# Expert passes rewritten: routing weights copied over the partitions by DMA, gate activated in its bank, norm on ScalarE, routing chain moved

## The chip, the cores and the metric

The kernel runs on one core of a Trainium2 chip. The core has TensorE (PE; its weight loads are listed as PEld), VectorE (DVE), ScalarE (ACT), GpSimd (POOL), SyncE (SP, which here only issues DMAs), 16 DMA engines, an SBUF of 128 partitions and a PSUM of 8 banks (128 partitions x 512 fp32 each). The metric is device time in microseconds of one execution; less is better.

## The reference

Six sublayers work on x, 4 x 1024 tokens of 128 features in fp32, each on a layer norm of x and added to x:

```python
x = x + 0.5 * L0_ffn(ln(x))    # pass ffn0a
x = x + L0_attn(ln(x))
x = x + 0.5 * L0_ffn(ln(x))    # pass ffn0b
x = x + 0.5 * L1_ffn(ln(x))    # pass ffn1a
x = x + L1_attn(ln(x))         # gated unit
x = x + 0.5 * L1_ffn(ln(x))    # pass ffn1b
```

The change is to the four expert passes. L0_ffn has 16 experts of 64 hidden units and a shared expert; L1_ffn has 8 experts of 256. Both compute every expert for every token and weight it by the router:

```python
# L0: scores = sigmoid(x @ gate_w.T); the best 2 of 4 groups, in them the best 4 experts
h = silu(x @ w1[e].T) * (x @ w3[e].T)
y = sum over e of comb[t, e] * (h @ w2[e].T)     # + shared expert, weight 1
# L1: softmax over 8 experts, the best 2, normalized; the same sum with w_gate, w_up, w_down
```

## The kernel before, in words

`phase_moe` (L184) is one pass. It takes the 4096 tokens in 8 groups of 512 (G). Tokens lie on the free axis, hidden units on the partitions, in chunks of 128: NC = 9 chunks in layer 0 (two experts a chunk; the last is the shared expert), 16 in layer 1 (two chunks an expert). Every fp32 product is made of three fp32r matmuls (high x high, high x low, low x high), so each operand is split in a high and a low half.

For chunk c of a group, `up_and_gate` (L302) has three matmuls for the gate, three for the up projection, and one more (L319): a constant selector `sel` times `combt`, the routing weights with experts on the partitions. It spreads each expert's weights over the partitions of its hidden units, in a PSUM bank; in layer 1 only each second chunk has it. ACT takes the silu of the gate from PSUM to SBUF (`silu`, L407); DVE multiplies it with the spread weights (`scale`, L606) and the up projection (`hide`, L614); ACT rounds the result to its high half (`high`, L415), POOL subtracts for the low half (`low`, L461); PE projects down with three matmuls, two chunks later (`project`, L323). ACT has `silu` of chunk c ahead of `high` of c-1. Gate, up and spread weights have two PSUM banks each, y one, and one bank, `misc`, serves every transpose.

Beside the chunks of group g runs a chain for group g+1: DVE's statistics (`stats`, `aggr`), POOL's reciprocal root (`invert`, L455), DVE's `norm` (L509), PE's `turn` (four transposes), ACT's `xh`, DVE's `xl`, the router's `logit` on PE, `lout` on ACT, `lturn` on PE, the selection `r1` to `r4` on DVE (with a tanh on ACT), PE's `cturn` and ACT's copy to `combt`. `r4` writes the weights in a high and a low half (`cstack`). For group g-1, `yout` (ACT), `yturn` (PE) and `add` (DVE, L598) bring y into x. Each engine's program is in order. The dictionary `slot` (L244) says behind which chunk each step of the chain stands; an instruction waits there if its input isn't ready. Groups 2 to 5 of a pass run in a hardware loop of two groups a turn.

SP is idle in the passes, but for weights of the next layer (`SplitAhead`, L1148: all pieces are loaded at the start of the pass; ACT and POOL split them in groups 0, 1, 6 and 7) and the stores of the last pass. In the attention SP copies rows of queries and keys from SBUF to SBUF: L1043 takes 32 rows of `att_parts`, three planes each, to 96 rows; L1057 8 rows, three planes, to 24 rows. In setup, `sel` is loaded and rounded by POOL (L163).

Of the kernel before, what the change touches and what calls it, by code (L numbers as in the profile page):

```python
# [34 lines left out]
ARENA = 13568  # L35
AHEAD = 704
# [7 lines left out]
def pack_layout():  # L44
    at, lay = 0, {}
    for name, n in (("ident", P), ("causal", P), ("causalT", P), ("qsign", 1), ("qlow", 1), ("ksign", 1),
                    ("klow", 1), ("kone", 1), ("outside", P), ("sel0", C0 * P), ("sel1", E1 * P),
                    ("cos", S), ("sin", S)):
        lay[name] = (at, at + n)
        at += n  # L50
    return lay, at

def constants():
# [46 lines left out]
def phase_setup(nc, k, t, a):  # L101
# [3 lines left out]
    with ExitStack() as ctx:  # L105
# [12 lines left out]
        raw_sel, raw_att = sb("raw_sel", [P, C0 * P]), sb("raw_att", [P, 3, P])  # L118
# [20 lines left out]
        def _(act):  # L139
# [4 lines left out]
            act.dma_start(raw_sel[:], a["consts"][:, slice(*lay["sel0"])]).then_inc(consts_in, 16)  # L144
# [9 lines left out]
            act.wait_ge(consts_in, 32)  # L154

        @block.gpsimd
        def _(pool):
# [4 lines left out]
            pool.wait_ge(consts_in, 32)  # L162
            pool.tensor_copy(k.sel[:], raw_sel[:])  # L163
# [5 lines left out]
        def _(dve):  # L169
# [10 lines left out]
            dve.wait_ge(consts_in, 32)  # L180
# [3 lines left out]
def phase_moe(nc, k, tag, layer, turn_no, ahead=None, out=None):  # L184

# [15 lines left out]
    with ExitStack() as ctx:
# [8 lines left out]
        st, mv, veps, rstd = sb("st", [P, TG, 6]), sb("mv", [P, TG, 2]), sb("veps", [P, TG]), sb("rstd", [P, TG])  # L211
        xn, xh_sb, xl_sb = sb("xn", [P, TG, D]), sb("xh", [P, 2, G], F32R), sb("xl", [P, 2, G], F32R)
# [4 lines left out]
        top_sb, pen, hs, df = (sb("top", [P, TG, 8]), sb("pen", [P, TG, 4]), sb("hs", [P, TG, 1]),  # L217
                               sb("df", [P, TG, E1]))
        cstack, combt = sb("cstack", [P, TG, P]), sb("combt", [P, 2, G], F32R)
        sil, scl, hid = sb("sil", [P, 2, G]), sb("scl", [P, 2, G]), sb("hid", [P, 2, G])  # L220
        hid_h, hid_l, y_t = sb("hid_h", [P, 2, G], F32R), sb("hid_l", [P, 2, G], F32R), sb("y_t", [P, G])

        gate_ps, up_ps, comb_ps = k.banks[:, 0:2, :], k.banks[:, 2:4, :], k.banks[:, 4:6, :]
        y_ps, misc = k.banks[:, 6, :], k.banks[:, 7, :]
        misc3 = misc[:].rearrange("p (t c) -> p t c", c=P)

# [4 lines left out]
        logits_t, logits_out, logits_turned, logits_read = (sem(s) for s in  # L231
            ("logits_t", "logits_out", "logits_turned", "logits_read"))
        route = sem("route")
        tanh_done = sem("tanh_done")
        comb_turned, comb_t = sem("comb_turned"), sem("comb_t")
        y_out, y_turned, y_added = sem("y_out"), sem("y_turned"), sem("y_added")

# [3 lines left out]
        comb_done, comb_high, stack_cleared = sem("comb_done"), sem("comb_high"), sem("stack_cleared")  # L241
        ROUTE = 12 if first else 8
# [10 lines left out]
        def place(g, c):  # L253

            near = {g0: 0, g0 + 1: 1, g0 + NG - 2: 2, g0 + NG - 1: 3}
            if ahead is None or not isinstance(g, int) or g not in near or c % 3 != 1 or c > 7:
                return None
            n = 3 * near[g] + c // 3
            return n if n < ahead.count else None

        if ahead is not None or out is not None:
            @block.sync
            def _(sp):
                if ahead is not None:
                    ahead.load(sp)
                if out is not None:
                    stored = sem("stored")
                    for g in range(NG):
                        sp.wait_ge(y_added, g0 + g + 1)
# [5 lines left out]
        def _(pe):  # L275
            def turn(g, q):
                pe.wait_ge(norm_done, g + 1)
                if not isinstance(g, int) or g > 0:
                    pe.wait_ge(comb_t, g)
# [1420 lines left out]
```

## Time and profile before

| | |
|---|---|
| time, median of 3 runs | 2032.54 us (2031.74 to 2033.6) |
| time of the profiled execution | 2030.13 us |
| its span, first to last instruction | 2028.2 us |
| busy: PE, DVE, ACT, POOL | 86%, 71%, 47%, 36% |
| mean granted TensorE clock | 0.944 of full speed |
| bytes moved by DMA | 28.08 MB |

The page has the busy time of each engine, the span in 40 slices, the DMA queues, the chain that ended last, and the costliest groups of instructions by source line. The names before `<-` are what is written, behind it what is read, without buffer numbers; `banks` is PSUM. A busy PE is a matmul under way; as matmuls overlap, their starts show the rate, not their durations. Idle time in brackets is that of the engine just before the instruction, with what ended it. In windows the last three numbers are the granted clock, the mean busy share of the 16 DMA engines and what they moved.

### The profile page before, as it was taken

To read this page: it belongs to the slowest core of one execution; us is meant where nothing else is said; L and a number is where in the kernel's file an instruction comes from. 1 tells how busy PE (TensorE), PEld (TensorE's weight loads), DVE (VectorE), ACT (ScalarE), POOL (GpSimd) and SP (SyncE) were. 2 spreads that over 40 slices of the span, in tenths; PEclk is the share of its full clock that TensorE was granted. 3 is DMA by queue.
4 is the path that set the end of the run, shared out by engine and by line. 5 is a ranking of instruction groups with operands and counts; after the bars stand their busy time and mean duration, and the time that the engine had idled before them with its cause. 6 is when DMAs were issued, how large, how long until landed. Compare 5 with 4: busy or idle time off the path is not lost. (4 is left out here: it accounts for less than half of the span.)

```text
span 2028.2 us, 28208 instructions
## 1 busy us (share of the span) xinstructions
PE 1744.3 (86%) x8712; PEld 1247.0 (61%) x8712; DVE 1439.9 (71%) x4268; ACT 960.2 (47%) x1557; POOL 729.4 (36%) x659
## 2 busy tenths in 40 slices
PE   3898959899899899977998799999967775999998
PEld 2666735555555555535766577777856564777776
DVE  5878748777777777827788567777667765677675
ACT  2444414565565555654444355555532221555554
POOL 3444421312312312124445455555521001555555
PEclk9999968999999999987999899999978887999999
DMA  3000011111111111010000100000000000000000
GB/s 103 1 1 0 1 29 22 26 22 27 21 22 30 18 22 28 12 39 37 0 1 0 40 1 1 1 0 0 1 0 0 0 1 1 1 11 6 5 11 11
DMA packets 18248, 28.08 MB, mean 14 GB/s; under 512 B 2753, under 2 KB 10178, under 8 KB 18130
## 3 DMA queue, kind: packets, MB, share of 16 engines
q1 hardware_dynamic: 15874, 23.68, 5.4%
q10 hardware_dynamic: 2256, 2.96, 0.5%
q8 instruction: 58, 0.95, 0.2%
q14 instruction: 60, 0.49, 0.1%
HBM read 10.83 MB, written 2.10 MB: 6 GB/s over the span
## 5 line engine op out<-in xcount | busy, mean ns | idle before, releaser
L976 ACT ACTIVATE att_probs<-banks 128x1024 f32<-128x1024 f32 (+3 forms) x384 | 305.9, 811 | 197.1 <-PE banks L887 195.3
L1101 DVE CUSTOM_DVE_ANT_0 banks<-banks,att_mask 128x128 f32<-128x128 f32 (+3 forms) x512 | 234.3, 525 | 73.5 <-PE banks L868 73.0
L868 PE MATMUL banks<-arena 128*128 128x512 f32 (+3 forms) x768 | 250.1, 407 | 27.5 <-DMA arena<-att_parts 15.1
L1016 POOL TENSOR_SCALAR_AFFINE_SELECT att_probs<-att_probs 128x512 f32<-128x512 f32 x128 | 81.2, 635 | 422.7 <-ACT att_probs L976 422.7
L868 PEld LDWEIGHTS banks<-arena 128*128 128x128 f32 x768 | 133.1, 198 | 151.6 <-issue 91.9
L461 POOL TENSOR_TENSOR ffn1b_hid_l<-ffn1b_hid,ffn1b_hid_h 128x512 fp32r<-128x512 f32 x128 | 165.0, 1292 | 130.0 <-ACT ffn1b_hid_h L415 130.0
L461 POOL TENSOR_TENSOR ffn1a_hid_l<-ffn1a_hid,ffn1a_hid_h 128x512 fp32r<-128x512 f32 x128 | 165.3, 1293 | 125.2 <-ACT ffn1a_hid_h L415 125.2
L887 PE MATMUL banks<-arena 128*128 128x512 f32 (+3 forms) x768 | 205.2, 352 | 0.5 <-ACT att_probs L976 0.4
L1103 DVE TENSOR_REDUCE att_mx<-banks 128x1 f32<-128x512 f32 x256 | 162.2, 684 | 32.0 <-PE banks L868 31.8
L906 PE MATMUL banks<-att_probs,att_v_aug 128*32 128x512 f32 (+3 forms) x1536 | 167.7, 509 | 0.6 <-POOL att_probs L1016 0.5
L887 PEld LDWEIGHTS banks<-arena 128*128 128x128 f32 x768 | 137.7, 191 | 26.4 <-ACT att_probs L976 11.3
L606 DVE TENSOR_TENSOR ffn1b_scl<-ffn1b_sil,banks 128x512 f32<-128x512 f32 x128 | 88.1, 688 | 81.8 <-PE banks L314 41.1
L606 DVE TENSOR_TENSOR ffn1a_scl<-ffn1a_sil,banks 128x512 f32<-128x512 f32 x128 | 88.0, 688 | 79.9 <-PE banks L314 39.2
L407 ACT ACTIVATE ffn1b_sil<-banks 128x512 f32<-128x512 f32 x128 | 76.5, 598 | 114.7 <-PE banks L309 112.0
L407 ACT ACTIVATE ffn1a_sil<-banks 128x512 f32<-128x512 f32 x128 | 76.4, 597 | 113.8 <-PE banks L309 111.1
L461 POOL TENSOR_TENSOR ffn0a_hid_l<-ffn0a_hid,ffn0a_hid_h 128x512 fp32r<-128x512 f32 x72 | 92.5, 1288 | 105.0 <-ACT ffn0a_hid_h L415 105.0
L461 POOL TENSOR_TENSOR ffn0b_hid_l<-ffn0b_hid,ffn0b_hid_h 128x512 fp32r<-128x512 f32 x72 | 92.5, 1286 | 98.2 <-ACT ffn0b_hid_h L415 98.2
L309 PE MATMUL banks<-ffn1b_xh,arena 128*128 128x512 f32 x256 | 104.2, 407 | 0.0
L309 PE MATMUL banks<-ffn1a_xh,arena 128*128 128x512 f32 x256 | 104.0, 406 | 0.0
L314 PE MATMUL banks<-ffn1b_xh,arena 128*128 128x512 f32 x256 | 102.4, 400 | 0.0
L314 PE MATMUL banks<-ffn1a_xh,arena 128*128 128x512 f32 x256 | 100.8, 394 | 0.0
L614 DVE TENSOR_TENSOR ffn1a_hid<-ffn1a_scl,banks 128x512 f32<-128x512 f32 x128 | 87.9, 687 | 6.3 <-POOL ffn1a_hid_l L461 1.8
(404 smaller groups left out, 4176.3 us busy)
## 6 DMA issues: line engine op xcount, KB each, us to landing
arena<-att_parts SPq DMA_DIRECT2D x16, 384.0 KB
arena<-att_parts SPq DMA_DIRECT2D x128, 48.0 KB
w_raw<-in_ffn_w_dram SPq DMA_DIRECT2D x6, 352.0 KB, 5.5
out_dram<-x SPq DMA_DIRECT2D x8, 256.0 KB, 2.3
setup_raw<-in_ffn_w_dram SPq DMA_DIRECT2D x3, 576.0 KB, 6.4
w_raw<-in_ffn_w_dram SPq DMA_DIRECT2D x3, 320.0 KB, 6.2
setup_raw_sel<-in_consts_dram ACTq DMA_DIRECT2D x1, 576.0 KB, 10.9
x<-in_L_attn_x_dram ACTq DMA_DIRECT2D x1, 512.0 KB, 8.0
```

The costliest lines, as they stand in the source:

```text
L309: mm = pe.matmul(gate_ps[:, n, :], w[:, ws], xx[:, q, :], start=m == 0, stop=m == 2)
L314: mm = pe.matmul(up_ps[:, n, :], w[:, ws], xx[:, q, :], start=m == 0, stop=m == 2)
L407: act.activation(sil[:, n, :], gate_ps[:, n, :], ACT.Silu).then_inc(silu_done, 1)
L461: pool.tensor_tensor(hid_l[:, n, :], hid[:, n, :], hid_h[:, n, :].bitcast(F32), ALU.subtract)\
L606: dve.tensor_tensor(scl[:, n, :], sil[:, n, :], comb_ps[:, comb_bank(q, c), :], ALU.mult).then_inc(scaled, 1)
L614: dve.tensor_tensor(hid[:, n, :], scl[:, n, :], up_ps[:, n, :], ALU.mult).then_inc(hidden, 1)
L868: mm = pe.matmul(bank[:, at:at + width], q_st[:, n % 3, t * P:(t + 1) * P], k_pad[:, n % 2, j, c * G:c * G + width], start=True, stop=True ...
L887: mm = pe.matmul(score_ps[:, pair, h, 0:c], k_pad[:, n % 2, 2 * pair + h, kb * P:(kb + 1) * P], q_st[:, n % 3, (qg + 1) * G - c:(qg + 1) * ...
L906: mm = pe.matmul(o_ps[32 * j:32 * j + 32, G - c:G], v_aug[:, b % 2, kb, at:at + 32], probs[:, unit % NPROB, j, 0:c], start=kb == 0, stop=k ...
L976: act.activation(probs[:, unit % NPROB, 2 * pair:2 * pair + 2, 0:c], score_ps[:, pair, :, 0:c], ACT.Exp, scale=SCALE).then_inc(exped, 1)
L1101: ins = dve.tensor_tensor_reduce(now, now, mask[:, G - width:G], 1.0, -3e38, ALU.add, ALU.max, best)
L1103: ins = dve.tensor_reduce(best, now, AX.X, ALU.max)
```

## The change

- The selector matmuls, `sel`, its load and rounding, and `cstack` go. `cturn` transposes `comb` itself to the NE rows of `combt`. SP copies row n of `combt` to all 128 partitions (layer 0: two rows, 64 partitions each) of `share[:, e, :]`, for 8 slots e, one semaphore each, one buffer each. `scale` waits for the semaphore and multiplies by `share`.
- `silu` writes to its own PSUM bank. `scale` reads it there. The shared expert's chunk has no scale; its silu goes to SBUF.
- Gate and up have three banks each, `hid` and its halves three buffers.
- `norm` goes from DVE to ACT, as x * rstd + nshift; POOL computes nshift behind the root.
- `slot` is changed; statistics and norm stand in the group before the last; the loops are unrolled.
- The penalty of the expert groups is written transposed, with a fifth column that nobody reads.
- `SplitAhead` loads its pieces (512 columns, 704 before) one by one into three buffers, in groups 1 to 7, two a group.

```diff
-    def comb_bank(q, c):
-        return (q * NC + c) // PER % 2
+    SLOTS = 8
+    NSCALED = SLOTS * PER
+    HALVES = P // I0 if first else 1
+    LAG = 2
+    NB, NH = 3, 3
...
+    if first:
+        slot = dict(stats=7, aggr=7, rstd=8, norm=8, turn=0, xh=0, xl=0, logit=2, lout=2, lturn=3,
+                    r1=3, r2=4, r3=5, r4=6, cturn=7, yout=2, yturn=5, y=5)
+    else:
+        slot = dict(stats=13, aggr=13, rstd=14, norm=14, turn=1, xh=1, xl=1, logit=3, lout=3, lturn=5,
+                    r1=5, r2=7, r3=9, r4=11, cturn=13, yout=2, yturn=7, y=8)
+    early = ("stats", "aggr", "rstd", "norm")
...
+    def chain(h, c, parts):
+
+        for name, f in parts:
+            g = h + (2 if name in early else 1)
+            if slot[name] == c and g0 <= g < end:
+                f(g)
...
-        if first:
-            slot = dict(stats=0, aggr=0, rstd=0, norm=1, turn=2, xh=2, xl=2, logit=3, lout=3, lturn=4,
-                        r1=4, r2=5, r3=6, r4=7, cturn=8, yout=2, yturn=6, y=7)
-        else:
-            slot = dict(stats=0, aggr=0, rstd=0, norm=2, turn=3, xh=3, xl=3, logit=5, lout=5, lturn=7,
-                        r1=7, r2=9, r3=11, r4=13, cturn=14, yout=2, yturn=9, y=10)
...
+            for g in range(g0, end):
+                sp.wait_ge(comb_t, g + 1)
+                for e in range(SLOTS):
+                    if g > g0:
+                        sp.wait_ge(scaled, (g - 1) * NSCALED + (e + 1) * PER)
+                    for h in range(HALVES):
+                        n, at = e * HALVES + h, h * P // HALVES
+                        sp.dma_start(share[at:at + P // HALVES, e, :],
+                                     combt[n:n + 1, g % 2, :].unsqueeze(1).broadcast_to([1, P // HALVES, G]))\
+                          .then_inc(share_in[e], 16)
+                if out is not None and g > g0:
+                    store(g - 1)
+                for c in range(NC):
+                    if piece_at(g + 1, c) is not None:
+                        ahead.load(sp, piece_at(g + 1, c))
...
+                at_least(pe, hidden, num - NB + 1)
...
-                if c % PER == 0:
-                    e = c // PER
-                    if c == 0:
-                        pe.wait_ge(comb_t, g + 1)
-                    mm = pe.matmul(comb_ps[:, comb_bank(q, c), :], sel[:, e * P:(e + 1) * P], combt[:, q, :],
-                                   start=True, stop=True)
...
+            def norm(g):
+                act.wait_ge(rstd_done, 2 * g + 2)
+                for t in range(TG):
+                    ins = act.activation(xn[:, t, :], k.x[:, tile_of(g, t)], ACT.Identity, bias=nshift[:, t:t + 1],
+                                         scale=rstd[:, t:t + 1])
+                ins.then_inc(norm_done, 1)
...
+                gate = gate_ps[:, num % NB, :]
+                act.activation(gate if c < NSCALED else sil[:], gate, ACT.Silu).then_inc(silu_done, 1)
...
                 pool.tensor_tensor(rstd[:], veps[:], k.neghalf[:, 0:TG], ALU.pow).then_inc(rstd_done, 1)
+                pool.wait_ge(rstd_done, 2 * g + 1)
+                pool.tensor_tensor(nshift[:], nmean[:], rstd[:], ALU.mult).then_inc(rstd_done, 1)
...
+            def scale(g, c):
+                num, n = g * NC + c, g * NSCALED + c
+                dve.wait_ge(silu_done, num + 1)
+                if c % PER == 0:
+                    dve.wait_ge(share_in[c // PER], (g + 1) * HALVES * 16)
+                dve.tensor_tensor(scl[:, num % 2, :], gate_ps[:, num % NB, :], share[:, c // PER, :], ALU.mult)\
+                   .then_inc(scaled, 1)
+                dve.wait_ge(scaled, n + 1)
...
+                    step(dve.tensor_scalar(pen[:].rearrange("p (e t) -> p e t", t=TG),
+                                           gmark[:, :, 0:5].rearrange("p t e -> p e t"), TAKEN, OUT, ALU.not_equal,
+                                           ALU.mult), g)
```

## Rows read from the trace of the kernel before

**Rows 1.** The page, part 1: busy us (share of the span) xinstructions.

```profile
PE 1744.3 (86%) x8712; PEld 1247.0 (61%) x8712; DVE 1439.9 (71%) x4268; ACT 960.2 (47%) x1557; POOL 729.4 (36%) x659
```

**Rows 2.** Windows of the four passes: us, busy of each engine, clock, DMA share, GB/s.

```profile
36.00:258.10 222.10, 197.33 (x859) 151.02 (x857) 168.50 (x522) 103.43 (x182) 99.30 (x79) 0.98 0.00 1
921.60:1152.60 231.00, 202.51 (x859) 154.92 (x857) 175.74 (x522) 110.13 (x193) 113.96 (x89) 0.95 0.00 1
1167.90:1485.50 317.60, 306.19 (x1355) 243.58 (x1353) 223.00 (x522) 164.16 (x296) 175.21 (x138) 0.99 0.00 1
1704.80:2028.20 323.40, 308.38 (x1355) 244.98 (x1353) 222.65 (x523) 162.89 (x293) 171.87 (x135) 0.98 0.02 7
sum 1094.10, PE 1014.40 PEld 794.50 DVE 789.89 ACT 540.62 POOL 560.35; mean PE 253.60 PEld 198.62 DVE 197.47 ACT 135.15 POOL 140.09
```

**Rows 3.** Line L309: ns min/median/max, first and last start us.

```profile
L309 PE MATMUL banks<-ffn0a_xh,wgh x72: 391/394/776, 35.9 to 250.4; 128*128 128x512 f32 x72
```

**Rows 4.** Timeline, PE, layer 0: start us, us, ... [idle before <-releaser].

```profile
156.28 0.47 PE L330 MATMUL banks<-ffn0a_hid_h,wdh 128*128 128x512 f32 x1 [0.48 <-POOL ffn0a_hid_l L461]
...
158.03 0.66 PE L281 MATMUL banks<-pack,ffn0a_xn 128*128 128x128 f32 x4 [0.82 <-DVE ffn0a_xn L509]
...
166.90 0.39 PE L309 MATMUL banks<-ffn0a_xl,wgh 128*128 128x512 f32 x1
167.14 0.39 PE L309 MATMUL banks<-ffn0a_xh,wgl 128*128 128x512 f32 x1
...
176.02 0.66 PE L299 MATMUL banks<-pack,ffn0a_cstack 128*128 128x128 f32 x4 [1.29 <-DVE ffn0a_cstack L590]
```

**Rows 5.** Timeline, ACT and POOL, one chunk of layer 0.

```profile
167.57 0.60 ACT L407 ACTIVATE ffn0a_sil<-banks 128x512 f32<-128x512 f32 x1 [1.22 <-PE banks L309]
...
168.06 0.62 ACT L415 ACTIVATE ffn0a_hid_h<-ffn0a_hid 128x512 fp32r<-128x512 f32 x1
...
168.76 1.28 POOL L461 TENSOR_TENSOR ffn0a_hid_l<-ffn0a_hid,ffn0a_hid_h 128x512 fp32r<-128x512 f32 x1 [1.04 <-ACT ffn0a_hid_h L415]
```

**Rows 6.** Timeline, DVE, the same group.

```profile
155.11 2.86 DVE L509 TENSOR_SCALAR ffn0a_xn<-x,ffn0a_mv,ffn0a_rstd 128x128 f32 x4
...
168.84 1.24 DVE L556 TENSOR_SCALAR ffn0a_pen<-ffn0a_gmark 128x16 f32<-128x16 f32 x1
```

**Rows 7.** Timeline, PE and POOL, layer 1.

```profile
1331.55 1.01 POOL L455 TENSOR_TENSOR ffn1a_rstd<-ffn1a_veps,neghalf 128x4 f32<-128x4 f32 x1 [1.41 <-DVE ffn1a_veps L504]
...
1332.52 2.52 POOL L461 TENSOR_TENSOR ffn1a_hid_l<-ffn1a_hid,ffn1a_hid_h 128x512 fp32r<-128x512 f32 x2
...
1333.94 0.47 PE L330 MATMUL banks<-ffn1a_hid_h,arena 128*128 128x512 f32 x1 [1.09 <-POOL ffn1a_hid_l L461]
```

**Rows 8.** Groups by line: busy us, mean ns, idle before, releasers.

```profile
L319 PE MATMUL banks<-ffn0b_combt,sel 128*128 128x512 f32 x72 | 29.2, 405 | 0.0
```

**Rows 9.** Windows: DMA into 128 rows; from 32 rows; from 8 rows.

```profile
7.00:9.00 2.00, 0.00 (x0) 0.00 (x0) 1.02 (x2) 1.16 (x1) 2.00 (x2) 1.00 1.02 401
401.00:402.00 1.00, 1.00 (x8) 0.95 (x8) 0.96 (x3) 0.29 (x1) 0.53 (x1) 1.00 0.91 184
417.50:421.00 3.50, 2.12 (x13) 0.49 (x11) 2.25 (x13) 1.41 (x3) 0.00 (x0) 1.00 0.39 56
```

**Rows 10.** DMA issues: KB each, median us to landing.

```profile
arena<-att_parts SPq DMA_DIRECT2D x16, 384.0 KB
arena<-att_parts SPq DMA_DIRECT2D x128, 48.0 KB
...
out_dram<-x SPq DMA_DIRECT2D x8, 256.0 KB, 2.3
```

**Rows 11.** Line L1057, its issue on SP: ns min/median/max.

```profile
L1057 SPq DMA_DIRECT2D arena<-att_parts x128: 665/673/1212, 281.1 to 841.3; - x128
```

**Rows 12.** Windows around a PE stall in layer 0.

```profile
144.30:147.70 3.40, 1.57 (x9) 0.93 (x8) 3.15 (x8) 0.63 (x1) 1.04 (x2) 1.00 0.00 0
147.70:151.10 3.40, 3.40 (x11) 2.71 (x10) 0.94 (x3) 1.71 (x3) 1.52 (x2) 0.54 0.00 0
```

More of the change, by code:

```diff
@@ L251, in phase_moe @@
-        block = ctx.enter_context(nc.Block())
[L253 to L269, printed above, removed]
-                        sp.dma_start(out.rearrange("b (n p) d -> p (b n) d", p=P)[:, g * TG:(g + 1) * TG, :],
-                                     k.x[:, g * G:(g + 1) * G].rearrange("p (n d) -> p n d", d=D)).then_inc(stored, 16)
-                    sp.wait_ge(stored, 16 * NG)
+        block = ctx.enter_context(nc.Block())
@@ L335, in yturn @@
                 pe.wait_ge(y_out, g + 1)
-                if more:
+                if g + 2 < end:
                     if first:
@@ L341, in yturn @@
                         pe.wait_ge(route, (g + 2) * ROUTE + 1)
+                elif g + 1 < end:
+                    pe.wait_ge(comb_t, g + 2)
+                else:
+                    pe.wait_ge(y_added, g)
                 for t in range(TG):
@@ L421, in yout @@
                 act.activation(y_t[:], y_ps, ACT.Copy).then_inc(y_out, 1)
[L423 to L424 removed]
+            for h in range(g0 - 2, end):
                 for c in range(NC):
[L426 to L439 removed]
@@ L451, in _ @@
+                    chain(h, c, (("norm", norm), ("xh", xh), ("lout", lout), ("r1", r1), ("r2", r2), ("cturn", cturn)))
+            high(end * NC - 1)
+            yout(end - 1)
         @block.gpsimd
@@ L464, in body @@
-            def body(g, q, more):
-                start = isinstance(g, int) and g == g0
-                for c in range(NC):
-                    if c > 0:
-                        low(g, q, c - 1)
-                    elif not start:
-                        low(g - 1, 1 - q, NC - 1)
-                    if place(g, c) is not None:
-                        ahead.low(pool, place(g, c))
-                    if more and slot["rstd"] == c:
-                        invert(g + 1)
+                pool.tensor_tensor(hid_l[:, num % NH, :], hid[:, num % NH, :], hid_h[:, num % NH, :].bitcast(F32),
+                                   ALU.subtract).then_inc(low_cut, 1)
@@ L616, in body @@
-            def body(g, q, more):
-                real = not (isinstance(g, int) and g < g0)
-                for c in range(NC):
-                    if real and slot["y"] == c and not (isinstance(g, int) and g == g0):
-                        add(g - 1)
-                    if real:
-                        scale(g, q, c)
-                        hide(g, q, c)
-                    if more:
-                        for s, f in (("stats", stats), ("aggr", aggr), ("norm", norm), ("xl", xl), ("r1", r1),
-                                     ("r2", r2), ("r3", r3), ("r4", r4)):
-                            if slot[s] == c:
-                                f(g + 1, 1 - q)
+                at_least(dve, low_cut, num - NH + 1)
@@ L638, in _ @@
-            body(g0, 0, True)
-            body(g0 + 1, 1, True)
-            with dve.Fori(1, NG // 2 - 1) as i:
-                body(g0 + 2 * i, 0, True)
-                body(g0 + 2 * i + 1, 1, True)
-            body(g0 + NG - 2, 0, True)
-            body(g0 + NG - 1, 1, False)
-            add(g0 + NG - 1)
+            for h in range(g0 - 2, end):
+                for c in range(NC):
+                    if h >= g0:
+                        if slot["y"] == c and h > g0:
+                            add(h - 1)
+                        if c < NSCALED:
+                            scale(h, c)
+                        hide(h, c)
+                    chain(h, c, (("stats", stats), ("aggr", aggr), ("xl", xl), ("r1", r1), ("r2", r2), ("r3", r3),
+                                 ("r4", r4)))
@@ L648, in parcel @@
+            add(end - 1)
 def parcel(arena):
@@ L1572, in weights @@
         def weights(layer, get):
[L1573 removed]
+            NC = C0 if layer == 0 else C1
             def ws(name, n):
```

419 lines of the change are left out of this document (175 added, 244 removed).

## The prediction

> **What bounds the kernel now.** I read the page's busy times first: PE 86% of a span of 2028.2 us, no other engine above 71% [rows 1]. Then the windows by stage. The four expert passes, each from its first gate matmul to its end, take 222.1, 231.0, 317.6 and 323.4 us, 1094.1 us together; PE is busy for 1014.4 of them, and the DMA share is 0.00 to 0.02 [rows 2]. The change touches these 1094 us and little else; the other 934 us (setup, attention, gated unit, starts of passes) stay. A pass has 8 groups of 512 tokens, so a group takes 27.8 us in layer 0 (222.1/8) and 39.7 us in layer 1 (317.6/8).
>
> Next the timeline of one group. Wide matmuls start 0.23 us apart (166.90 to 167.14) [rows 4]. Layer 0 has 10 a chunk: 9 x 10 x 0.233 = 21.0 us, plus three for the logits and 16 short transposes, about 23.4; the other 4 us are waits, for the low half of POOL (0.48), the normed tokens of DVE (0.82) and the routing weights (1.29) [rows 4]. The normed tokens are late because four small DVE instructions take 2.86 us beside POOL [rows 6]. In layer 1, with 9.5 matmuls a chunk, the waits are about 1.5 us a group, the largest where POOL computes the reciprocal root (1.01 us) ahead of the low halves and PE waits 1.09 us [rows 7]. So PE is the bound, with one chain right behind it: silu to high half 0.49, to low half 0.70, low half 1.28 [rows 5], then projection and the gate two chunks on. With some 0.15 us into the projection, 5 matmul pitches and 0.43 to the next silu (167.14 to 167.57) that is 4.2 us per two chunks.
>
> **The change part by part.**
>
> *Matmuls out.* 72+72+64+64 = 272 selector matmuls go, three forms alike [rows 8]: 272 x 0.233 = 63 us of PE. A chunk is then 9 x 0.233 = 2.10 us, and the chain above needs 4.2/2 = 2.1: all of it can come back, with no slack left.
>
> *Routing weights by DMA.* This is the large term. In place of each selector matmul SP copies one row of combt to 128 rows of share: 128 x 2 KB = 256 KB a slot, 8 slots and 2 MB a group, 64 MB in all, where the kernel before moved 28 MB. In layer 0 a slot is two DMAs with 64 destination rows, in layer 1 one. The issue costs SP 0.67 us each [rows 11], 10.8 us a group at most, beside everything else on an idle queue. The transfer reads all 256 KB from one row (two neighbouring rows in layer 0). The trace has no such copy, so I bound it by what there is: loads that fill 128 rows ran at 401 GB/s with the 16 engines full (share 1.02); the 384 KB copy out of 32 rows at 184 GB/s with a share of 0.91; the 48 KB copies out of 8 rows at 56 GB/s with a share of 0.39 [rows 9, 10]. Busy engines moved half as much when they read 32 rows, though those packets went to 96 rows, so the source is what narrows. Per source row that is 184/0.91/32 = 6.3 GB/s; as one rate for any small source it is 56. Ends of the price of a slot: 256 KB at 401 GB/s, 0.65 us, and at 6.3 GB/s, 42 us. I take 26.5 GB/s, near what four neighbouring rows had in both copies (202/8 = 25, 56/2 = 28): the nearest rows leave no sign that one row gets more than its neighbours had together. A slot then takes 262,144/26.5e3 = 9.9 us.
>
> By the Trainium skill (SBUF — State Buffer, "Door 1: The DMA port swizzle"), DMA bandwidth depends on how many of 16 ports the partitions reach; four neighbours share one, at about 27.2 GB/s each. It speaks against this change: one source row reaches one port. By its figure a slot takes 9.6 us and the sum below would end near 3460 us. The trace agrees where it can: 32 rows, 8 ports, 202 GB/s full.
>
> What waits: DVE's scale of chunk c waits for its slot, and behind it on DVE stand hide, the layer norm statistics, the router's steps and the add; ACT's high half, POOL's low half and PE's projection follow. Three banks let PE run two chunks ahead, no more. Can the queue stay full across groups? The next group's weights need r4 (slot 6, or 11), which stands behind the scale that uses share 6 (or 5); its transpose is at slot 7 (or 13). So comb_t comes about 3 us after share 6 lands, while share 7 still has 7 us to go, and SP queues the next group's slots behind it. The pass then runs at the rate of the queue: 8 x 9.9 = 79 us a group, against 27.8 and 39.7. Eight groups: 633 us; plus 2.3 us until a first landing [rows 10] and the tail after the last share, about 9 us (7.7 now from the last gate matmul, 250.4, to the end, 258.1 [rows 2, 3]): 644 us a pass. Sixteen weight pieces and eight stores of 256 KB now share the full queue, 0.65 us each: 15 us.
>
> *Gate activated in its bank, three banks each.* The silu reads PSUM as before (0.60 us, [rows 5]) and writes there instead of SBUF; between -0.1 and +0.2 us each, no matter behind the share wait; nothing taken. Chunk 8 of layer 0 skips its scale: 16 x 0.69 of DVE, hidden.
>
> *Norm from DVE to ACT, one more POOL multiply.* DVE loses 2.86 us (layer 0, [rows 6]) a group. But ACT now has high half 7, then the norm, in one slot, and the norm needs POOL's low half (1.28), root (1.01) and a multiply (none in the trace; 0 to 1.01, I take 0.5). ACT so stands about 3.1 + 0.5 us after the high half starts, then four small instructions of at most 0.49 (I take 0.2): the next silu comes 2.7 us late (4.9 for 2.1 after its predecessor). Behind it wait all high halves. Without a DMA bound this costs PE 2.4 us (layer 0; the transposes give 0.35 cover) to 2.7 us a group; under 79 us a group it is hidden.
>
> *Routing chain moved up; the penalty step.* In layer 0 the penalty's layout is changed; that step took 1.24 us beside POOL [rows 6]. The transpose of the result and DVE's add now share slot 5: DVE holds scale 5 until PE has transposed, about 1 us, and r3 follows; some 1.7 us a group if PE were the bound. Both hidden here; so are the two dropped copies of the weights.
>
> *Setup, loops.* 576 KB of selectors are not loaded: at most 1.4 us at 401 GB/s, against it two more small instructions ahead of each pass's first norm. Unrolled loops cost nothing visible: repeated groups took what unrolled ones do. I take 0 for both, within 5 us either way.
>
> **Sum.** 2028.2 - 1094.1 + 4 x 644 + 15 = 3525 us of span. The profiled run took 2030.1, 1.9 more than its span, and lies 2.4 under the median of 2032.5; so 3525 within a unit of rounding, and 3520 is my forecast.
>
> **The rivals.**
>
> *B: a small source gives about 56 GB/s whatever its rows.* A slot is 4.7 us, a group 37.4: layer 0 goes from 27.8 to 37.4, layer 1 stays at its own 39 to 40. 16 x 9.6 + 5 = 159: about 2190 us. For it: the 8-row rate was seen with engines at 0.39, so it may have been short of requests. Against: the 32 rows.
>
> *C: the copy is not in the way, and the kernel gets faster.* It decides at the pace of the scales: 25.5/8 = 3.2 us a slot in layer 0, a rate of 82 GB/s, and 4.9 us in layer 1. Then PE is the bound again. Layer 0: 84 wide matmuls 19.6, transposes 1.8, norm stall 2.4, add stall 1.7: 25.5, 2.3 less than 27.8. Layer 1: 147 x 0.233 = 34.3, transposes 1.8, norm 2.7, tanh's wait 0.5: 39.3, 0.4 less. 16 x 2.7 = 43, less some 10 for starts of passes: about 2000 us. For it: one row is a short read that engines might serve at the 401 of rows 9. Against: the copies out of SBUF in rows 9, both below.
>
> *D: C, but the norm stall costs clock.* In one stretch PE was busy for 1.57 of 3.40 us, at a granted clock of 1.00; in the stretch behind it the clock was 0.54, near 1.2 GHz instead of 2.4 [rows 12]. A stall of 2.7 us in every group could bring that to most: 1.7 us each, 32 times, 54 us: 2050 us.
>
> *E: 6.3 GB/s for the one row*, 42 us a slot, near 11,900 us. Eight readers of one row slower than of several; nothing but a division supports it.
>
> **How the numbers follow.** A 0.51, with its own range 3400 (27.5 GB/s) to 3750 (24.6); B 0.10; C 0.27; D 0.09; E 0.03. Below A lie more than two tenths, so the range must reach to C: 1970 to 3750 leaves out E and the tails. About 0.2% (4 us) is what a measurement tells from none. Faster: C but 0.02, so 0.25. Same: 0.03 with D's lower edge. Slower: 0.72.
>
> **What would show it.** In the passes a DMA share near 1.0 at 24 to 28 GB/s, groups 77 to 84 us apart in both layers, PE busy for about a third, and DVE's scale waiting for the DMA of share, by far the longest wait; SP's wait on comb_t short. Attention and the gated unit as before. If the share of the DMA engines is below 0.5 in layer 0 and the scale waits for the silu, A and B are wrong; then the wait of ACT's norm for POOL, once a group, tells whether the 2.7 us are there, and the granted clock in those windows tells C from D. A slot faster than 4.9 us but above 3.2 gives a layer 0 that is slow and a layer 1 that is not.

## The result and the profile after

The changed kernel takes 3230.86 us (median of 4 runs, 3228.8 to 3235.06), the kernel before 2032.76 in the same job: ratio 1.5897, 95% interval 1.5869 to 1.5924. Predicted were 3520 us, own range of that case 3400 to 3750, range 1970 to 3750. It is case A, some 290 us milder than worked out: 3230.86 lies below A's own range and inside the whole one, which had been stretched down to 1970 for the cases B to D.

The page of the changed kernel: busy times against [rows 1], the slices of clock, DMA share and GB/s, the queue, the chain that ended last, and the issues with the time to landing, which stand against [rows 10].

```profile
PE 2061.4 (64%) x8440; PEld 1415.8 (44%) x8440; DVE 1366.7 (42%) x4086; ACT 1002.9 (31%) x1687; POOL 729.5 (23%) x693
...
PEclk8667676599999996666666788888878878888888
DMA  6888888211111105888888688888850048888887
GB/s 73 32 32 32 31 32 32 29 22 22 22 24 23 24 12 18 35 43 37 38 38 34 37 36 29 30 29 30 29 20 1 0 13 32 31 32 33 33 33 30
...
q1 hardware_dynamic: 55074, 90.29, 64.1%
...
DMA 16%; SPq 1%; DVE 1%; PE 0%; ACT 0%; issue 0%; POOL 0%; DVEq 0%
...
ffn0b_share<-ffn0b_combt SPq DMA_DIRECT2D x128, 128.0 KB, 15.6
ffn1a_share<-ffn1a_combt SPq DMA_DIRECT2D x64, 256.0 KB, 30.1
...
out_dram<-x SPq DMA_DIRECT2D x8, 256.0 KB, 21.6
```

In the four passes the DMA engines are busy for 0.86 of the time and move only 30 to 36 GB/s; an output store that took 2.3 us takes 21.6, as it stands in the same queue as the copies of share. The windows of the four passes, each from its first gate matmul, as in [rows 2]:

```profile
34.10:580.30 546.20, 284.25 (x787) 199.20 (x785) 137.55 (x476) 111.20 (x210) 99.50 (x86) 0.68 0.86 31
1241.40:1800.80 559.40, 289.98 (x787) 202.34 (x785) 137.65 (x478) 117.40 (x223) 114.72 (x99) 0.66 0.86 36
1815.60:2403.70 588.10, 374.54 (x1291) 278.43 (x1289) 223.30 (x485) 174.29 (x324) 174.94 (x145) 0.84 0.86 30
2624.00:3227.50 603.50, 385.27 (x1291) 284.46 (x1289) 223.46 (x485) 173.35 (x321) 171.60 (x142) 0.83 0.86 32
sum 2297.20, PE 1334.04 PEld 964.43 DVE 721.96 ACT 576.24 POOL 560.75; mean PE 333.51 PEld 241.11 DVE 180.49 ACT 144.06 POOL 140.19
```

The passes grew from 1094.1 to 2297.2 us; the rest of the span went from 934.1 to 930.3. So the whole loss, 1203 us, is inside the passes. PE's busy time rose with fewer matmuls, as the granted clock fell to 0.66 to 0.68 in layer 0 and 0.83 to 0.84 in layer 1 (0.95 to 0.99 before): in the stretch 2705.5 to 2710 us, at 0.50 (1.2 GHz), a wide matmul is listed with 0.63 us, at 1.00 with 0.40.

The groups by line of the changed kernel (busy, mean ns of one, idle before and what ended it) name the wait: DVE's scale, for share.

```profile
L551 DVE TENSOR_TENSOR ffn0b_scl<-banks,ffn0b_share 128x512 f32<-128x512 f32 x64 | 44.3, 692 | 410.4 <-DMA ffn0b_share<-ffn0b_combt 410.4
L551 DVE TENSOR_TENSOR ffn1b_scl<-banks,ffn1b_share 128x512 f32<-128x512 f32 x128 | 88.0, 687 | 365.6 <-DMA ffn1b_share<-ffn1b_combt 363.0
```

And DVE's timeline gives the pace, first in layer 1, where each slot of 256 KB serves two chunks (the second is left out), then in layer 0:

```profile
2701.50 0.69 DVE L551 TENSOR_TENSOR ffn1b_scl<-banks,ffn1b_share 128x512 f32<-128x512 f32 x1 [2.60 <-DMA ffn1b_share<-ffn1b_combt]
...
2711.45 0.69 DVE L551 TENSOR_TENSOR ffn1b_scl<-banks,ffn1b_share 128x512 f32<-128x512 f32 x1 [7.22 <-DMA ffn1b_share<-ffn1b_combt]
...
2721.40 0.69 DVE L551 TENSOR_TENSOR ffn1b_scl<-banks,ffn1b_share 128x512 f32<-128x512 f32 x1 [6.61 <-DMA ffn1b_share<-ffn1b_combt]
...
2730.66 0.69 DVE L551 TENSOR_TENSOR ffn1b_scl<-banks,ffn1b_share 128x512 f32<-128x512 f32 x1 [6.52 <-DMA ffn1b_share<-ffn1b_combt]
...
2736.61 0.69 DVE L551 TENSOR_TENSOR ffn1b_scl<-banks,ffn1b_share 128x512 f32<-128x512 f32 x1 [2.67 <-DMA ffn1b_share<-ffn1b_combt]
```

```profile
282.89 0.69 DVE L551 TENSOR_TENSOR ffn0a_scl<-banks,ffn0a_share 128x512 f32<-128x512 f32 x1 [7.22 <-DMA ffn0a_share<-ffn0a_combt]
...
289.24 0.69 DVE L551 TENSOR_TENSOR ffn0a_scl<-banks,ffn0a_share 128x512 f32<-128x512 f32 x1 [2.84 <-DMA ffn0a_share<-ffn0a_combt]
...
299.05 0.69 DVE L551 TENSOR_TENSOR ffn0a_scl<-banks,ffn0a_share 128x512 f32<-128x512 f32 x1 [6.91 <-DMA ffn0a_share<-ffn0a_combt]
...
305.96 0.69 DVE L551 TENSOR_TENSOR ffn0a_scl<-banks,ffn0a_share 128x512 f32<-128x512 f32 x1 [5.36 <-DMA ffn0a_share<-ffn0a_combt]
```

Layer 1 reads: 9.95, 9.95, 9.26, 5.95 us from slot to slot (the last row is slot 3). Layer 0: 6.35 (slot 5), 9.81, 6.91 (slot 7). Most slots take 9.5 to 10.1 us, about the 9.9 forecast (262,144 bytes in 9.95 us are 26.3 GB/s, in 9.6 us, the usual time in layer 1, 27.3); slots 3 and 7 in layer 1 (mostly 5 to 9.4 us) and all odd ones in layer 0 (5.4 to 9.3) are short. These are the slots whose source row is the last in a group of four neighbouring rows of combt: layer 1 reads 8 rows in 8 slots, layer 0 16. A group of eight slots comes to 66 to 72 us in layer 0 and 69 to 77 us in layer 1, from gate matmul to gate matmul.

The rate shows the same. These are the GB/s of the changed kernel in layer 0, between 100 and 200 us, in slices of 2.5 us:

```profile
GB/s 27 39 29 28 27 27 27 30 29 52 27 27 26 26 34 48 40 25 26 26 26 34 57 26 30 26 26 28 43 29 27 26 27 27 34 44 43 26 26 25
```

It stands at 25 to 30, and rises to 39 to 57 about every 17 us. Each rise ends about where an odd slot lands (123.7, 140.8, 156.7, 173.1 us), which is where the queue changes from one group of four rows to the next. A rate of up to twice that of one group says that for some microseconds both are read at once.

### The profile page after: what moved, and what is told of

Read it like the earlier page. It is cut to its first block and busy times, and to the rows that moved or that the text cites. A ratio compares the mean times of both kernels' runs of the same rounds, so it can differ in the third digit from the quotient of the medians.

```text
span 3227.5 us, 26274 instructions
## 1 busy us (share of the span) xinstructions
PE 2061.4 (64%) x8440; PEld 1415.8 (44%) x8440; DVE 1366.7 (42%) x4086; ACT 1002.9 (31%) x1687; POOL 729.5 (23%) x693
## 5 line engine op out<-in xcount | busy, mean ns | idle before, releaser
L399 ACT ACTIVATE banks<-banks 128x512 f32<-128x512 f32 x384 | 223.1, 581 | 252.2 <-PE banks L317 251.9
L551 DVE TENSOR_TENSOR ffn1b_scl<-banks,ffn1b_share 128x512 f32<-128x512 f32 x128 | 88.0, 687 | 365.6 <-DMA ffn1b_share<-ffn1b_combt 363.0
L551 DVE TENSOR_TENSOR ffn1a_scl<-banks,ffn1a_share 128x512 f32<-128x512 f32 x128 | 88.0, 688 | 353.6 <-DMA ffn1a_share<-ffn1a_combt 343.7
L329 PE MATMUL banks<-ffn1b_hid_h,arena 128*128 128x512 f32 x128 | 71.6, 560 | 214.1 <-POOL ffn1b_hid_l L436 214.1
L329 PE MATMUL banks<-ffn1a_hid_h,arena 128*128 128x512 f32 x128 | 70.6, 551 | 212.8 <-POOL ffn1a_hid_l L436 206.4
L799 PEld LDWEIGHTS banks<-arena 128*128 128x128 f32 x768 | 133.2, 198 | 151.2 <-issue 92.0
L329 PE MATMUL banks<-ffn0b_hid_h,wdh 128*128 128x512 f32 x72 | 49.5, 687 | 212.9 <-POOL ffn0b_hid_l L436 212.9
L329 PE MATMUL banks<-ffn0a_hid_h,wdh 128*128 128x512 f32 x72 | 47.2, 656 | 200.0 <-POOL ffn0a_hid_l L436 200.0
L404 ACT ACTIVATE ffn0b_hid_h<-ffn0b_hid 128x512 fp32r<-128x512 f32 x72 | 45.1, 627 | 401.6 <-DVE ffn0b_hid L561 401.6
L404 ACT ACTIVATE ffn0a_hid_h<-ffn0a_hid 128x512 fp32r<-128x512 f32 x72 | 45.2, 628 | 395.0 <-DVE ffn0a_hid L561 393.3
## 6 DMA issues: line engine op xcount, KB each, us to landing
out_dram<-x SPq DMA_DIRECT2D x8, 256.0 KB, 21.6
```

The lines of the kernel that those rows point to most:

```text
L329: pe.matmul(y_ps, down_h[:, ws], hid_h[:, num % NH, :], start=c == 0, stop=False)
L399: act.activation(gate if c < NSCALED else sil[:], gate, ACT.Silu).then_inc(silu_done, 1)
L404: act.activation(hid_h[:, num % NH, :], hid[:, num % NH, :], ACT.Copy).then_inc(high_cut, 1)
L551: dve.tensor_tensor(scl[:, num % 2, :], gate_ps[:, num % NB, :], share[:, c // PER, :], ALU.mult)\
L799: mm = pe.matmul(bank[:, at:at + width], q_st[:, n % 3, t * P:(t + 1) * P], k_pad[:, n % 2, j, c * G:c * G + width], start=True, stop=True ...
```

## The experiments

Theory: the copy of share is held at its source, since all its bytes come out of one group of four neighbouring SBUF rows; all else of the change hides under that. Rivals: the number or size of the DMAs, the writing side, a limit of the single row, and other parts of the change that cost as well.

**1. Each destination row from a row of its own.** Same DMAs, bytes and waits, other source rows.

```
-  combt[n:n + 1, g % 2, :].unsqueeze(1).broadcast_to([1, P // HALVES, G])
+  fixed[at:at + P // HALVES, :]
```

> The share tile is filled by the same 64 to 128 DMAs a group, the same bytes and the same waits, but each destination row is read from the row of the same number of a fixed tile (all 0.125), instead of all from one row of combt. The weights are thereby a constant, so the output is not the routed one; everything else of the changed kernel runs. Theory (the reads are held by the one source row, 31.5 GB/s in layer 0 and 29 GB/s in layer 1): the wait for share disappears, groups fall from 68 us to about 25.5 us in layer 0 and from 70-76 us to about 39.3 us in layer 1, and the kernel takes about 2000 us (1980 to 2060). Rival (the DMAs are held by their number, their sizes of 2 KB a row, their issue or the writing side, all of which stay): about 3230 us, groups 66 to 76 us. What the time ends at under the theory is also the price of the rest of the change: with the norm stall of 2.4 us a group or a lower clock it is 2050 us.

Measured: 2012.91 us (2007.14 to 2017.75), ratio to before 0.9905 [0.9881, 0.9928]. The wait for share is gone from the scale, a landing takes 2.3 us, and while copies run the engines move about 205 GB/s. The writing side, the issue and the number of DMAs are cleared.

**2 and 3. Four source rows, neighbours or four apart.**

```
e2:  fixed[0:4, :].unsqueeze(1).broadcast_to([4, P // HALVES // 4, G])
e3:  fixed[0:16:4, :].unsqueeze(1).broadcast_to([4, P // HALVES // 4, G])
```

> As the run with a fixed source tile, but every DMA of a share half or whole reads rows 0 to 3 of the fixed tile, each 16 (layer 0) or 32 (layer 1) times. Constant weights, so not the routed output. If the limit belongs to a single row, four rows carry four times as much, about 110 GB/s or 2.3 us a slot, and the time is about 2000 us. If four neighbouring rows share one limit, it stays at 27 to 31 GB/s, 8.3 to 9.9 us a slot and 3200 to 3500 us.

> As the run with four neighbouring source rows, but the four rows are 0, 4, 8 and 12. Constant weights, so not the routed output. Under either form of the source-row theory four rows in four different groups of four carry about four times as much: 2.3 to 2.5 us a slot, about 2000 us. If it is the number of different rows in a wider sense (any four rows are too few, or a DMA of few source rows is served by few engines), it stays above 5 us a slot and 2500 us. The difference between this run and the one with neighbouring rows is the size of the group of rows that shares a limit.

Measured, one run each: 3720.44 us with rows 0 to 3, 2032.07 us with rows 0, 4, 8 and 12. The two kernels differ in one stride. The first is slower than the 3200 to 3500 expected, since that range took over the rate of the changed kernel, overlaps at its changes of rows included; here there are none. A window of each in layer 0, neighbours first (the last three numbers: clock, DMA share, GB/s), and the GB/s slices of the second between 100 and 200 us:

```profile
100.00:700.00 600.00, 249.82 (x684) 175.67 (x685) 122.83 (x431) 95.70 (x182) 86.90 (x75) 0.65 0.24 25
```

```profile
DMA  2221002222222200222222231012222222200222
GB/s 98 97 97 64 0 25 98 97 101 105 98 98 98 97 37 2 100 98 98 98 97 97 98 93 67 2 42 99 98 98 97 98 97 98 97 12 10 76 98 98
```

**4. The real weights, by way of DRAM.**

```
+  sp.dma_start(scratch[g % 2], combt[:, g % 2, :]).then_inc(scratch_in, 16)
+  sp.wait_ge(scratch_in, 16 * (g + 1))
-  combt[n:n + 1, g % 2, :].unsqueeze(1).broadcast_to([1, P // HALVES, G])
+  scratch[g % 2, n].partition_broadcast(P // HALVES)
```

> The real computation. Once a group combt (8 or 16 rows of 2 KB) is copied to DRAM, and the 8 slots of share are then filled from there, each row of share from the same 2 KB of DRAM. Theory (the limit is in reading one SBUF row): the DRAM reads are not held by it, the extra step costs one DMA of 2 to 4 us a group that lies beside matmuls for most of its length, and the time is 2000 to 2080 us. Rival 1 (all rows from one 2 KB line are slow wherever it lies, or the writing side holds them): 3000 us or more. Rival 2 (the two DMAs in a row come too late for the first scale of each group): 4 us more for each of 32 groups, 2130 us.

Measured: 2017.40 us (2012.44 to 2024.41), ratio 0.9928 [0.9910, 0.9946]; the copies land in 3.0 us (128 KB) and 4.6 to 4.8 us (256 KB). One source line of 2 KB is no hindrance in DRAM. Against the changed kernel 1213 us are back.

**5. The real weights out of SBUF, expert n on row 4n.**

```
-  comb[:, t, :]  ->  misc[0:NE, ...];  source combt[n:n + 1, g % 2, :]
+  comb[:, t, ::4] filled, rest 0  ->  misc[0:4 * NE, ...];  source combt[4 * n:4 * n + 1, g % 2, :]
```

> The real computation with the transfer still out of SBUF, but the weights of expert n lie on row 4n of combt, so no two experts share a group of four rows (the transposes and the copy widen from 8 or 16 rows to 32 or 64). Theory (four neighbouring rows share 24.4 GB/s, as the run with four neighbouring source rows shows, and the changed kernel was at 31.5 GB/s in layer 0 and 29 GB/s in layer 1 because transfers on both sides of a change of four rows overlap): the more changes, the faster. Between two slots the gain seen at a change was some 4.5 us of 21.4 (layer 0) and 6.4 us of 42.8 (layer 1), so at least 5 to 6 us a slot, groups of 40 to 50 us in both layers, and 2250 to 2550 us; if more than two transfers overlap, down to 2020 us. Rival (each source row has the limit, neighbours do not matter): unchanged, 3230 us.

Measured, one run: 2291.25 us. Groups last mostly 34 to 40 us in layer 0, below the 40 to 50 expected, and 45 to 46 in layer 1, inside it. Two windows, 200 us in layer 0 and 300 in layer 1:

```profile
100.00:300.00 200.00, 145.05 (x536) 103.57 (x534) 99.70 (x372) 76.72 (x145) 68.34 (x59) 0.88 0.83 56
1340.00:1640.00 300.00, 259.52 (x1088) 196.65 (x1088) 182.87 (x433) 146.07 (x273) 148.17 (x123) 0.96 0.80 49
```

56 GB/s are about twice what one group of four gave: by this reckoning some two transfers are read at a time, not eight. The short slots of the changed kernel fit that, with their rises to 57 GB/s: the last slot of four rows runs beside the start of the next one, which reads elsewhere. How the queue shares out the engines was not measured by itself, so that is argued and not shown.

**6 and 7. What the rest of the change costs: the norm stall.** Run 4 shows what the share wait had covered. Its timelines at the end of a group in layer 1, ACT, POOL and PE:

```profile
1341.11 0.63 ACT L408 ACTIVATE ffn1a_hid_h<-ffn1a_hid 128x512 fp32r<-128x512 f32 x1
1344.39 1.65 ACT L373 ACTIVATE ffn1a_xn<-x,ffn1a_nshift,ffn1a_rstd 128x128 f32<-128x128 f32 x4 [2.65 <-POOL ffn1a_nshift L436]
1345.95 0.57 ACT L403 ACTIVATE banks<-banks 128x512 f32<-128x512 f32 x1
...
1341.82 1.30 POOL L440 TENSOR_TENSOR ffn1a_hid_l<-ffn1a_hid,ffn1a_hid_h 128x512 fp32r<-128x512 f32 x1 [1.33 <-ACT ffn1a_hid_h L408]
1343.07 1.02 POOL L434 TENSOR_TENSOR ffn1a_rstd<-ffn1a_veps,neghalf 128x4 f32<-128x4 f32 x1
1344.16 0.20 POOL L436 TENSOR_TENSOR ffn1a_nshift<-ffn1a_nmean,ffn1a_rstd 128x4 f32<-128x4 f32 x1
...
1345.12 0.40 PE L324 MATMUL banks<-ffn1a_xh,arena 128*128 128x512 f32 x1
1348.47 0.79 PE L333 MATMUL banks<-ffn1a_hid_h,arena 128*128 128x512 f32 x1 [2.96 <-POOL ffn1a_hid_l L440]
```

ACT's normalization waits for POOL's low half, power and multiply, and holds up what comes behind it on ACT; the next silu, high half and low half come late, and PE idles 2.96 us. The windows of run 4 before, in, and after the stall show the clock:

```profile
1337.00:1343.70 6.70, 6.70 (x32) 5.08 (x31) 5.06 (x17) 2.88 (x6) 4.47 (x4) 1.00 0.08 24
1343.70:1348.40 4.70, 1.81 (x8) 1.13 (x6) 1.81 (x3) 3.56 (x8) 1.83 (x3) 0.93 0.91 310
1348.40:1354.40 6.00, 5.93 (x16) 4.66 (x17) 2.24 (x4) 1.35 (x3) 2.58 (x3) 0.50 0.23 85
```

After the gap PE runs at 0.50 (1.2 GHz) for 6 us. So it goes behind 11 of the 12 such gaps of run 4 in layer 1. In layer 0 the gap is 2.07 us long, and the clock falls behind 7 of 12; around one of them, where the stretch behind was granted 0.60:

```profile
1012.00:1017.30 5.30, 5.20 (x25) 3.59 (x23) 4.99 (x16) 2.33 (x4) 3.27 (x3) 1.00 0.09 27
1017.30:1019.60 2.30, 0.28 (x2) 0.00 (x0) 0.00 (x0) 1.65 (x5) 0.53 (x2) 1.00 0.54 195
1019.60:1022.00 2.40, 2.35 (x9) 1.97 (x10) 1.86 (x3) 1.78 (x4) 1.28 (x1) 0.60 0.67 210
```

So the norm was moved to where DVE and ACT have slack, and in run 7 layer 0's routing chain one slot up as well:

```
-  layer 0: stats=7, aggr=7, rstd=8, norm=8      layer 1: stats=13, aggr=13, rstd=14, norm=14
+  layer 0: stats=1, aggr=1, rstd=2, norm=4      layer 1: stats=3, aggr=3, rstd=4, norm=6
run 7 only, layer 0:
-  logit=2, lout=2, lturn=3, r1=3, r2=4, r3=5, r4=6, cturn=7
+  logit=1, lout=1, lturn=2, r1=2, r2=3, r3=4, r4=5, cturn=6
```

> The kernel with the weights through DRAM, and the statistics, the power and the normalization of the group after next moved from the last slots of a group (7, 7, 8, 8 in layer 0; 13, 13, 14, 14 in layer 1) to 1, 1, 2, 4 and 3, 3, 4, 6. Theory: the power on POOL and the wait of the normalization on ACT behind it stop PE for 3.0 us at each end of a group (silu 15 comes behind the normalization), and in layer 1 PE then runs 14 matmuls at 0.43 us each instead of 0.23. Gone, this is worth 2 to 2.5 us a group in layer 0 and 5 us in layer 1: 2017 - 14 x 2.3 - 14 x 5 = 1915 us (1890 to 1950). Rival 1 (the stall moves along with the chain, since the power takes 1.0 us on POOL wherever it stands and ACT waits for it): 2010 to 2025 us. Rival 2 in layer 0 (the share DMAs, issued after slot 7, are then late for the first scale by 1 to 2 us): 15 us of the gain are lost, 1930 us.

> As the run before, and in layer 0 the routing chain one slot earlier (logits 1, their transposes and the first step 2, then 3, 4, 5, transposes of the weights 6), so that the DMAs start one slot (2.4 us) earlier. If the first scale of a group waits for share in layer 0 in the run before, this one is 1 to 2 us a group faster there, 15 to 30 us in all; if it does not, the two agree within 5 us, or this one is slower by the logits that now come only one slot after the cut of x.

Measured: 1948.51 us (1943.32 to 1950.38), ratio 0.9568 [0.9542, 0.9594], and 1928.23 us (1920.91 to 1933.87), ratio 0.9465 [0.9436, 0.9494]. Run 6 gained 69 us where about 100 were expected: layer 1 groups fell from 41.7 to 37.5 us, 4.2 instead of 5. In layer 0, 24.2 us for 26.1; there rival 2 came true. (1948.5 is just inside the 1890 to 1950 expected, 33 us over its centre.) The scale's waits in layer 0 of run 6, then of run 7:

```profile
L555 DVE TENSOR_TENSOR ffn0b_scl<-banks,ffn0b_share 128x512 f32<-128x512 f32 x64 | 44.0, 687 | 38.5 <-DMA ffn0b_share<-ffn0b_scratch 29.5 <-ACT banks L403 8.0
```

```profile
L555 DVE TENSOR_TENSOR ffn0b_scl<-banks,ffn0b_share 128x512 f32<-128x512 f32 x64 | 44.1, 689 | 27.7 <-DMA ffn0b_share<-ffn0b_scratch 16.0 <-ACT banks L403 10.9
```

Starting the copies a slot earlier halves the wait for share (29.5 to 16.0 us), groups fall to 22.4 and 23.1 us, and run 7 is 20 us faster than run 6. It is the best version, 5.3% under the kernel before.

**8. Two banks each.** `NB = 2` in run 6.

> As the run with the early normalization, with two PSUM banks each for gate and up instead of three. It prices the third bank. If the third bank carries the gain (gates start two slots ahead of hide), each slot is 0.2 to 0.4 us longer, as 2.4 us against 2.1 us a slot, and the time is 70 to 120 us more than with three. If the engines are paced by PE's matmuls alone, the two agree within 10 us.

Measured, one run: 1942.48 us, against 1943.32 to 1950.38 with three. The third bank is worth nothing in run 6.

**9 to 12. The transfer alone undone.** The copies of share go, and one selector matmul a slot into two banks comes back (silu to SBUF, two banks each for gate and up). Runs 9 and 11 are the changed kernel with that, 10 and 12 run 7 with it. In 9 and 10 selector and weights have 64 rows, in 11 and 12 128, as before the change.

```
-  dve.wait_ge(share_in[c // PER], (g + 1) * HALVES * 16);  gate_ps * share[:, c // PER, :]
+  pe.matmul(comb_ps[:, e % 2, :], sel[:, e, :], combt[:, g % 2, :], start=True, stop=True)
+  dve.wait_ge(up_done, num + 1);  sil * comb_ps[:, c // PER % 2, :]
```

> The changed kernel with the transfer alone undone: the weights come to the partitions by one selector matmul a slot into two PSUM banks, as before the change (high and low parts stacked in 64 rows, silu written to SBUF since the multiplication can read only one operand from PSUM, two banks each for gate and up); all else as changed, the normalization at the end of a group too. Theory (the share DMA alone made the kernel slow): all of 1200 us come back. The matmul adds 8 x 0.23 us a group, or 59 us in 32 groups, to the kernel with DRAM as source (2017 us) wherever PE is the bound, less where it waits anyway: 2020 to 2080 us. Rival (something else of the change costs too, and hid behind the DMA): over 2100 us. Rival (the spread by matmul is no dearer, since PE has room): 2000 to 2020 us.

> As the run before, with the normalization early and layer 0's routing chain one slot earlier: the kernel of 1928 us with the selector matmul in place of the DRAM round trip. It prices the idea of the change where nothing else is in its way. If PE is the bound (its matmuls are back to back for most of a group), the selector costs 8 x 0.23 = 1.8 us a group, 59 us, and the time is 1985 us (1960 to 2000). If the waits for the share DMA that are left (44 us before the scale, in four passes) and the DMA's load weigh as much, the two agree within 10 us.

Measured: 2108.93 us (2108.85 to 2109.34), ratio 1.0396 [1.0378, 1.0413], and 2033.50 us (2032.21 to 2039.19), ratio 1.0021 [1.0006, 1.0037]. Both lie above the theory's values, 29 and 33 us over their upper ends, and run 9 where the first rival had it. But what costs is in the new matmul itself. PE's timeline of run 10 shows why, at one selector matmul (L318):

```profile
1307.32 0.39 PE L313 MATMUL banks<-ffn1a_xl,arena 128*128 128x512 f32 x1
1307.55 0.40 PE L313 MATMUL banks<-ffn1a_xh,arena 128*128 128x512 f32 x1
1307.88 0.49 PE L318 MATMUL banks<-ffn1a_combt,ffn1a_sel 64*128 64x512 f32 x1
1308.30 0.50 PE L327 MATMUL banks<-ffn1a_hid_h,arena 128*128 128x512 f32 x1
1308.63 0.40 PE L328 MATMUL banks<-ffn1a_hid_h,arena 128*128 128x512 f32 x1
```

From start to start 0.23, 0.33, 0.42, 0.33: 0.4 us too much about one 64-row matmul among 128-row ones. It is so at all 256 of them: the three steps around one come to 1.08 us (median), and to 0.69 in run 11.

> As the run with the selector back, with the selector and the transposed weights on 128 rows (the rows in between are zero), as the kernel before the change has them, instead of 64. In the 64-row run the matmul of 64 rows between two of 128 rows took 0.32 + 0.43 + 0.33 us from start to start around it where the kernel before shows 0.23 us each: 0.63 us a slot instead of 0.23. Theory (the change of row number costs PE 0.4 us a slot): 8 x 0.4 = 3.2 us a group come back, up to 100 us in 32 groups where PE is the bound, less in groups with the stall: 2020 to 2050 us. Rival (the 64 rows are not the cause): 2109 us.

> As the run before, with the normalization early and layer 0's routing one slot earlier: a 128-row selector matmul where the kernel of 1928 us has the DRAM round trip. Theory: 2033.5 us less 3.2 us in each of 32 groups is 1931 us at best; with the waits that then show up on DVE and ACT, 1940 to 1985 us. It shows what the transfer is worth against the cheapest selector: 8 x 0.23 x 32 = 59 us if PE alone sets the time (1985 us), nothing if DVE and ACT do (1930 to 1940 us). Rival (the 64 rows are not the cause): 2033 us.

Measured: 2037.72 us (2031.45 to 2042.15), ratio 1.0026 [1.0008, 1.0045], and 1958.85 us (1956.07 to 1959.52), ratio 0.9643 [0.9621, 0.9666]. The same place in run 11:

```profile
1301.12 0.39 PE L313 MATMUL banks<-ffn1a_xh,arena 128*128 128x512 f32 x1
1301.35 0.39 PE L318 MATMUL banks<-ffn1a_combt,ffn1a_sel 128*128 128x512 f32 x1
1301.58 0.39 PE L327 MATMUL banks<-ffn1a_hid_h,arena 128*128 128x512 f32 x1
```

0.23 us throughout; 71 and 75 us came back, of 102 at most (32 x 3.2). Without the transfer the changed kernel is at 1.0026 of before: nothing else in it costs or gains much in sum. That sum hides two parts, for with norm and routing moved it is at 0.9643 (run 12): what the rest of the change gains, the norm stall takes back. And the spreading by DMA, fed from DRAM, beats the 128-row selector by 20 us with the norm stall (2037.7 to 2017.4) and by 31 without (1958.9 to 1928.2), half of PE's 59 us.

## Why the prediction was right, and where it was off

*The bound.* Right, and shown: changing nothing but the source takes 1213 to 1218 us off (runs 1 and 4). The choice between 401, 56 and 26.5 GB/s was made on the reasoning that 32 source rows, not the number of requests, had narrowed the copies of [rows 9]. Runs 2 and 3 confirm it for groups of four. E (6.3 GB/s for one row) fell: one row got what four get.

*The size.* The mis-sized term is "a slot then takes 262,144/26.5e3 = 9.9 us", taken for every slot. It measured mostly 9.3 to 10.2 us for the first slots of four rows and 5 to 9 for the last, as transfers overlap there. The mean is 8.5 us in layer 0 and 9.2 in layer 1, the passes sum to 2297.2 us instead of 2576 + 15. That accounts for the miss, and it is why A's own range, 3400 to 3750, was missed too. The prediction named layer 0's two neighbouring rows and did not follow them through the eight slots. It also gave both layers 79 us a group; layer 0, with twice as many changes of rows, has 68.

*DMA share near 1.0 at 24 to 28 GB/s.* 0.86 at 30 to 36: the dips and the rest are the overlaps. PE busy for a third: 0.52 to 0.64. With PE's busy times in run 4 (184.5 and 307.3 us a pass) it would be 0.34 in layer 0, but 0.52 in layer 1, which has more matmuls; the rest is the clock of 0.66 to 0.84, at which they last longer.

*Full queue across groups.* Held: the weights were ready 3.2 us (layer 0) and 2.6 us (layer 1) after scale 6 had its share, about the 3 forecast, and the first slot of a group comes mostly 9.5 to 10.2 us after the last one of the group before, as within a group. Stores took 21.6 us to land for the same reason. One sign was wrong: SP's wait for the weights was not short, some 15 us a group in ffn1a (105.6 us, 7 times). It cost nothing, since copies that take 30 us from issue to landing were still under way.

*Weight pieces.* The 15 us counted 16 pieces of 256 KB; the page lists 12. In ffn0b, where they are loaded, the first slot of a group took 10.6 to 11.5 us instead of 9.8 to 10.0 in ffn0a, so about the 2 x 0.65 us that were priced.

*Everything else hidden.* Right in the changed kernel; the silu in its bank took 581 ns of 598 before. As rival C had priced it, with no share wait: a norm stall of 2.4 and 2.7 us, where PE idled 2.07 and 2.96, and groups of 25.5 and 39.3 us, where run 1 has mostly 25.5 to 26.5 and 41.7 to 42.9. C missed the clock, which D had at 1.7 us a group: it falls in both layers. In layer 1 that is most of the 2.4 us over C's 39.3 (16 matmuls took 6.0 us at 0.50, and would take 3.7 at 0.233 us each); in layer 0 it is made up by stalls that were smaller than C had them. So the truth lies between C's 2000 and D's 2050: 2013. The add stall of 1.7 us in layer 0 was 0.75 at most.

*Attention and gated unit unchanged.* Held (934.1 to 930.3 us outside the passes).

*Chances.* C's condition, 82 GB/s, is met by sources that spread one DMA over several groups of four rows (205 GB/s in run 1, 98 in run 3) and by DRAM (310 GB/s in a window of run 4 above); it is not met where each DMA reads a single group of four, be it always the same (25, run 2) or another each time (56, run 5). The 0.27 was for a property of the source on which the copies of the kernel before already bore.

## What to carry to other kernels

Before a row is spread over the partitions by DMA, count the groups of four neighbouring SBUF rows that the source of each DMA covers: here each gave 24 to 27 GB/s, whatever the number of engines. A detour through DRAM (8 or 16 rows of 2 KB a group) removed 1213 us; rows spread over the groups, but still one a DMA, removed 940. When a new wait covers a whole stage, price what it covers anyway: here a stall of 3 us a group and the clock behind it were worth more (69 us) than the matmuls that the change set out to save. A source row that is moved costs one line to test, and a time of one run tells.

## What the runs showed of the hardware

- Four neighbouring SBUF rows as a source: 24.4 GB/s with four of them read (run 2), 26.3 to 27.3 with one (the changed kernel); four rows in four such groups: 98 GB/s, by as few engines (run 3).
- A DMA engine's busy share says nothing of its rate: 0.86 at 31 GB/s (the changed kernel), 0.24 at 25 (run 2), two tenths at 98 (run 3).
- With each DMA's source row in another group of four, one queue moved 56 GB/s (run 5), about twice the rate of one group, though eight slots were free.
- A matmul with 64 rows between matmuls with 128 costs PE about 0.6 us instead of 0.23 (runs 9 and 10); filled up with zeros to 128 rows it costs 0.23 (runs 11 and 12). What in PE does it was not tried.
